# Attention and mixture of experts on one core: TensorE's work of a head pair in two rounds by array form instead of four

## The chip, the core and the metric

The kernel runs on one core of a Trainium2 chip. The metric is the device time of one execution in microseconds, given as the median over several runs. TensorE does the matrix products and writes to PSUM; VectorE, ScalarE and GpSimd read PSUM or SBUF and do the rest; SyncE issues the DMAs. Each engine takes its own instructions in the order in which they are written, and semaphores order the engines against each other. In the profile TensorE is PE, its loads of stationary operands PEld, VectorE DVE, ScalarE ACT, GpSimd POOL, SyncE SP.

## The reference

Eight sequences of 512 tokens with 128 channels go through one post-norm layer: 16 heads of width 64, then eight experts of which the router takes two.

```
q, k, v = (einsum('bsd,hdk->bhsk', x, w) for w in (w_q, w_k, w_v))
weights = softmax(einsum('bhqk,bhmk->bhqm', q, k) / 8)
z = einsum('bhqm,bhmk->bhqk', weights, v)          # heads side by side, then z @ w_o
x = layernorm(x + (x + z @ w_o))
combine = softmax of the two largest of x @ gate_w, 0 elsewhere
y = sum over e of combine[e] * (silu(x @ w1[e]) @ w2[e])
out = layernorm(x + (x + y))
```

## The kernel before

**Tiling.** Two heads form a pair, one in the partitions 0 to 63 and one in 64 to 127; 8 sequences by 8 pairs of heads make 64 pairs, n = 0 to 63. Attention runs over the pairs (the first eight and last four written out, the rest in a loop of four); the experts follow. An operand of a product is mostly a high and a low part in fp32r, so that a product is three passes. For a pair TensorE does, with the lines of its matmuls:

- `coarse(n, u, t)`, L497: the high parts of q against k, for the queries of block t (t = 0 to 3), into the two PSUM banks COARSE and COARSE+1. VectorE's `maxima(n, t)`, L961, takes the maxima out of them; there is one such pair of banks, so block t+1 waits for the maxima of block t.
- `turn_maxima(n)`, L503: a transpose of the 128x128 maxima into bank COARSE. VectorE's `shift_part(n)`, L969, makes the shift out of it.
- `scores(n, u, t)`, L521 and L527: six products of q and k for the keys of block t, and two that add the shift, into the banks 0, 1 (t even) or 2, 3 (t odd). ScalarE's `exps`, L809, turns them into probabilities.
- `times_v(n, u, c)`, L539: block c of the probabilities times v, into bank Z. `sum_probs(n)`, L552: the sums of the probabilities, by a matrix of ones, into bank MISC. Both are float32.
- `project_q(n)`, `project_k(n)`, L447 to L449: q and k of a later pair, into bank MISC; `project_v(n)`, the same lines with an xT_cur operand, v of two pairs at a time, in even pairs only, into the banks 0 and 1; `project_out(n)`, the same lines with zT_hi, the output projection, into bank MISC.

**Array forms.** The profile writes the part of TensorE's array that a matmul uses, contraction by output: coarse and scores are 64\*128 (two heads in two halves of the rows, issued as a couple, and they run side by side), times_v and sum_probs are 128\*64 (two halves of the columns), the projections and the transpose are 128\*128.

**Order around the change.** In the pass of pair n TensorE does the scores of n, coarse of n+1, times_v and sum_probs of n-1, project_q and project_k of n+2, and project_out of n-2. A list in `body` (L595 to L625) sets their order by hand. The other engines have lists of their own, which name the same steps. VectorE's list for a pass is:

```
maxima(n + 1, 0)
reciprocals(n - 1)
maxima(n + 1, 1)
q_part(n + 2, (u + 2) % TURNS)
maxima(n + 1, 2)
maxima(n + 1, 3)
k_part(n + 2, (u + 2) % TURNS)
shift_part(n + 1)
z_part(n - 1)
acc_part(n - 2)
```

`reciprocals(n - 1)` (L977 to L981: a transpose of the sums out of bank MISC into zT, a reciprocal, a transpose back) waits for `sums_done` and for `zT_lo_done`, the step that last reads zT. That is GpSimd's `zT_part(n - 2)`, L363, the first step of GpSimd's pass, before its three additions of probabilities (L359). It takes what ScalarE's `zT_part(n - 2)`, L816, wrote, and ScalarE does that one right behind the first exponential of its pass (`exps(n, j, 0)`, `zT_part(n - 2)`, `exps(n, j, 1)`, `q_part`, `exps(n, j, 2)`, `k_part`, `exps(n, j, 3)`, and `v_part` in even pairs). `q_part` and `k_part` exist on ScalarE (high part, L790 and L794) and on VectorE (low part, L948 and L953).

Of the kernel before, what the change touches and what calls it, by code (L numbers as in the profile page):

```python
# [34 lines left out]
def attention_moe_kernel(nc, x, w_q, w_k, w_v, w_o, gate_w, w1, w2, out):  # L35
# [17 lines left out]
    with ExitStack() as ctx:  # L53
# [3 lines left out]
        def sem(name):  # L57
            return ctx.enter_context(nc.semaphore(name))
# [59 lines left out]
        def carve(*shape):  # L118

            n = 1  # L120
            for d in shape:
                n *= d
            ap = free[:, carved[0]:carved[0] + n]
            carved[0] += n
            names = " ".join("abc"[:len(shape)])
            return ap.rearrange(f"p ({names}) -> p {names}", **dict(zip("abc", shape))) if len(shape) > 1 else ap
# [3 lines left out]
        before = carve(NE, NE)  # L130
# [32 lines left out]
        s = {n: sem(n) for n in names}  # L163
# [4 lines left out]
        def wait(eng, semaphore, value):  # L168

            if not isinstance(value, int) or value > 0:  # L170
                eng.wait_ge(semaphore, value)
# [45 lines left out]
        def is_first(n):  # L217
            return isinstance(n, int) and n == 0
# [9 lines left out]
        def is_last(n, ahead):  # L228
            return isinstance(n, int) and n + ahead >= PAIRS
# [205 lines left out]
        def _(pe):  # L435
# [20 lines left out]
            def project_q(m, i, j):  # L456

                if isinstance(m, int) and m < 2:
                    pe.wait_ge(s["w_split"], 1)
                    wait(pe, s["k_hi_done"], m)  # L460
                    wait(pe, s["k_lo_done"], m)
                else:
                    pe.wait_ge(wqk_cur_in[j], DMA * i)

                    pe.wait_ge(s["k_hi_done"], m)
                    pe.wait_ge(s["k_lo_done"], m)
                    wait(pe, s["sums_out"], m - 2)
                project_qk(0, m, j).then_inc(s["q_done"], 1)

            def project_k(m, j):  # L470
                if isinstance(m, int) and m < 2:
                    pe.wait_ge(s["w_split"], 2)

                pe.wait_ge(s["q_hi_done"], m + 1)
                pe.wait_ge(s["q_lo_done"], m + 1)
                project_qk(1, m, j).then_inc(s["k_done"], 1)

            def project_v(m):

                pe.wait_ge(s["xT_cur_in"], DMA * (m // 2 + 1))  # L480

                pe.wait_ge(s["exp_done"], TT * m + 3)
                for t in range(TT):
                    tok = slice(t * P, (t + 1) * P)
                    mm = product(psum[:, t // 2, t % 2 * 2 * P:(t % 2 + 1) * 2 * P], [xT_cur[:, part, tok] for part in range(2)],
                                 [w_tab[:, bass.ds(m % HP, 2), 2, part, :] for part in range(2)])
                mm.then_inc(s["vT_done"], 1)

            def coarse(n, u, t):

                if t == 0:
                    pe.wait_ge(s["q_hi_done"], n + 1)
                    pe.wait_ge(s["k_hi_done"], n + 1)
                wait(pe, s["max_done"], TT * n + t)
                for h in range(2):
                    half = slice(h * DK, (h + 1) * DK)
                    mm = nc.tensor.matmul(psum[:, COARSE + h, :], q_pair[u][half, 0, t * P:(t + 1) * P],  # L497
                                          k_pair[u][half, 0, :], start=True, stop=True)
                mm.then_inc(s["coarse_done"], 1)

            def turn_maxima(n):
                pe.wait_ge(s["max_done"], TT * (n + 1))
                nc.tensor.transpose(psum[:, COARSE, 0:P], bits(neg_max[:]), ident[:]).then_inc(s["maxT_done"], 1)  # L503

            def scores(n, u, t):

                if is_first(n) and t == 0:
                    pe.wait_ge(s["xT_lo_done"], B)
                    pe.wait_ge(s["acc_set"], B // 2)
                    pe.wait_ge(s["ones_set"], 1)  # L510
                if t == 0:
                    pe.wait_ge(s["q_lo_done"], n + 1)
                    pe.wait_ge(s["k_lo_done"], n + 1)
                wait(pe, s["exp_done"], TT * n + t - 1)
                if t == 0 and u % 2 == 1:
                    pe.wait_ge(s["v_done"], (n - 1) // 2 + 1)
                keys = slice(t * P, (t + 1) * P)
                for kp, qp in ((0, 0), (1, 0), (0, 1)):
                    for h in range(2):
                        half = slice(h * DK, (h + 1) * DK)  # L520
                        nc.tensor.matmul(psum[:, 2 * (t % 2) + h, :], k_pair[u][half, kp, keys], q_pair[u][half, qp, :],  # L521
                                         start=(kp == 0 and qp == 0), stop=False)
                if t == 0:
                    pe.wait_ge(s["shift_done"], n + 1)
                for h in range(2):
                    half = slice(h * DK, (h + 1) * DK)
                    mm = nc.tensor.matmul(psum[:, 2 * (t % 2) + h, :], ones_r[half, :],  # L527
                                          shift[half].rearrange("p t q -> p (t q)"), start=False, stop=True)
                mm.then_inc(s["scores_done"], 1)

            def times_v(n, u, c):

                if c == 0:

                    pe.wait_ge(s["exp_done"], TT * n + TT)
                    pe.wait_ge(s["v_done"], (n - u % 2) // 2 + 1)
                    wait(pe, s["z_done"], n)
                for h in range(2):
                    mm = nc.tensor.matmul(psum[h * DK:(h + 1) * DK, Z, :], v[u // 2][:, u % 2, c, h, :], probs[u % 2][:, h, c, :],  # L539
                                          start=(c == 0), stop=(c == TT - 1))  # L540
                if c == TT - 1:
                    mm.then_inc(s["pv_done"], 1)

            def sum_probs(n):

                pe.wait_ge(s["added"], (TT - 1) * (n + 1))

                pe.wait_ge(s["k_hi_done"], n + 3 if not is_last(n, 2) else PAIRS)
                pe.wait_ge(s["k_lo_done"], n + 3 if not is_last(n, 2) else PAIRS)
                wait(pe, s["acc_done"], n - 1)  # L550
                for h in range(2):
                    mm = nc.tensor.matmul(psum[h * DK:(h + 1) * DK, MISC, :], ones, probs_sum[:, h, :], start=True, stop=True)  # L552
                mm.then_inc(s["sums_done"], 1)
# [28 lines left out]
            for t in range(TT):  # L582
                coarse(0, 0, t)
# [5 lines left out]
            def body(n, u):  # L589
                j = u % 2  # L590
                ahead, project = not is_last(n, 1), not is_last(n, 2)
                former, before_former = not is_first(n), not (isinstance(n, int) and n < 2)
                after, before = (u + 1) % TURNS, (u - 1) % TURNS

                scores(n, u, 0)  # L595
                if ahead:
                    coarse(n + 1, after, 0)
                if former:
                    times_v(n - 1, before, 0)
                    sum_probs(n - 1)  # L600
                scores(n, u, 1)
                if ahead:
                    coarse(n + 1, after, 1)
                if former:
                    times_v(n - 1, before, 1)
                if project:
                    project_q(n + 2, (n + 2 - j) // 2, j)
                scores(n, u, 2)
                if ahead:
                    coarse(n + 1, after, 2)  # L610
                if former:
                    times_v(n - 1, before, 2)
                if project:
                    project_k(n + 2, j)
                if ahead:
                    coarse(n + 1, after, 3)
                scores(n, u, 3)
                if j == 0:
                    project_v(n)
                if former:  # L620
                    times_v(n - 1, before, 3)
                if ahead:
                    turn_maxima(n + 1)
                if before_former:
                    project_out(n - 2)  # L625

            loops(pe, body)

            def to_tokens(b):
# [598 lines left out]
```

## Time and profile before

| | us |
|---|---|
| median of 3 runs | 1229.1 |
| lowest and highest | 1227.48 and 1229.37 |
| the profiled execution, its own time | 1227.94 |
| its span in the profile | 1226.1 |

The span is the time from the first to the last recorded instruction; 1.8 us lie around it. The pass of an odd pair takes some 13.2 us and that of an even pair, which holds `project_v`, some 14.7 us; pairs fill the span from about 35 to 925 us, the experts the rest. In a row of the timeline the first two numbers are start and duration in us; "x6" are matmuls of one line that follow each other. The matmuls are pipelined and their ends are modelled, so that a row's duration overlaps the next row: the time that a step costs TensorE is the distance from its start to the start of what follows. A bracket at the end of a row gives the engine's idle time before it and what released it.

### The profile page before, as it was taken

The page shows a single profiled execution, that of the slowest core. Times are in us where ns is not written, and L with a number is a line of the kernel's source. Part 1 is how long each engine was busy: PE and PEld are TensorE (multiplying, and loading weights), DVE is VectorE, ACT ScalarE, POOL GpSimd, SP SyncE. Part 2 cuts the span into 40 slices and gives each one's busy share as a digit, 9 for nine tenths or more (in the row PEclk, how much of TensorE's full clock was granted, in tenths as well). Part 3 has the DMA queues.
Part 4 walks back from the last instruction along what each step waited for, and adds up shares of the span by engine and source line. Part 5 has one row for each costly group of instructions (what it writes and reads, how often), then busy time and mean ns, then how long its engine had stood idle before and what let it go on. Part 6 is the DMA issues. An engine that isn't in the chain of part 4 may idle for free. (4 is left out here: it accounts for less than half of the span.)

```text
span 1226.1 us, 18385 instructions
## 1 busy us (share of the span) xinstructions
PE 1149.8 (94%) x5912; PEld 630.2 (51%) x5912; DVE 830.1 (68%) x1170; ACT 584.1 (48%) x680; POOL 728.8 (59%) x376
## 2 busy tenths in 40 slices
PE   4899999999999999999999999999996788988886
PEld 3444445444444444544444444455443666766664
DVE  4666866667766676666676766766765676677764
ACT  4445444444444444444444444444442556555653
POOL 0476766555666566665566655666565466566665
PEclk9999999999999999999999999999999899999999
DMA  7203111111111111111111111111100000000000
GB/s 171 73 19 103 44 44 44 43 56 43 43 43 45 66 47 43 43 43 56 43 43 43 43 64 52 43 43 43 48 26 35 1 9 18 18 17 17 9 10 18
DMA packets 41326, 52.31 MB, mean 43 GB/s; under 512 B 9296, under 2 KB 27728, under 8 KB 41296
## 3 DMA queue, kind: packets, MB, share of 16 engines
q1 hardware_dynamic: 41296, 51.92, 12.2%
q8 instruction: 17, 0.28, 0.1%
q14 instruction: 13, 0.11, 0.0%
HBM read 6.30 MB, written 2.10 MB: 7 GB/s over the span
## 5 line engine op out<-in xcount | busy, mean ns | idle before, releaser
L961 DVE TENSOR_REDUCE neg_max<-psum 128x2 fp32r<-128x1024 f32 x256 | 311.5, 1217 | 95.7 <-PE psum L497 93.9
L521 PE MATMUL psum<-q_pair,k_pair 64*128 64x512 f32 x1536 | 240.4, 417 | 3.7 <-DVE xT L943 2.6
L809 ACT ACTIVATE probs_even<-psum 128x1024 f32<-128x1024 f32 x128 | 131.2, 1025 | 164.4 <-PE psum L527 164.4
L809 ACT ACTIVATE x_tok<-psum 128x1024 f32<-128x1024 f32 x128 | 131.1, 1024 | 159.1 <-PE psum L527 159.1
L394 POOL TENSOR_TENSOR k_pair<-x_tok,q_pair 128x1024 fp32r<-128x1024 f32 x64 | 152.3, 2390 | 90.2 <-ACT q_pair L904 90.2
L359 POOL TENSOR_TENSOR probs_sum<-probs_sum,probs_even 128x1024 f32<-128x1024 f32 x64 | 152.6, 2384 | 64.8 <-ACT probs_even L809 64.7
L359 POOL TENSOR_TENSOR probs_sum<-probs_sum,x_tok 128x1024 f32<-128x1024 f32 x64 | 152.7, 2386 | 64.1 <-ACT x_tok L809 63.8
L521 PEld LDWEIGHTS psum<-q_pair,k_pair 64*128 64x128 f32 x1536 | 130.0, 185 | 117.0 <-issue 97.1
L363 POOL TENSOR_TENSOR zT_lo<-zT,zT_hi 128x512 fp32r<-128x512 f32 x64 | 82.4, 1287 | 125.3 <-ACT zT_hi L816 125.3
L539 PE MATMUL psum<-probs_even,v 128*64 128x512 f32 x512 | 138.1, 618 | 0.0
L539 PE MATMUL psum<-x_tok,v 128*64 128x512 f32 x512 | 137.9, 618 | 0.0
L1143 DVE TENSOR_TENSOR x_tok<-x_tok,psum 128x1024 f32<-128x1024 f32 x64 | 77.9, 1217 | 77.3 <-PE psum L685 48.4
L359 POOL TENSOR_TENSOR probs_sum<-probs_even 128x1024 f32<-128x1024 f32 x32 | 76.5, 2392 | 79.6 <-ACT probs_even L809 79.6
L497 PE MATMUL psum<-k_pair,q_pair 64*128 64x512 f32 x512 | 110.7, 427 | 5.3 <-DVE neg_max L961 5.3
L977 DVE STREAM_TRANSPOSE zT<-psum 128x512 f32<-128x512 f32 x64 | 45.9, 717 | 96.1 <-POOL zT_lo L363 95.4
L359 POOL TENSOR_TENSOR probs_sum<-x_tok 128x1024 f32<-128x1024 f32 x32 | 76.7, 2396 | 48.4 <-ACT x_tok L809 48.4
L527 PE MATMUL psum<-shift,ones_r 64*128 64x512 f32 x512 | 101.7, 391 | 0.0
L969 DVE TENSOR_TENSOR shift<-psum,shift_mask 128x512 fp32r<-128x512 f32 x64 | 44.3, 692 | 75.1 <-PE psum L503 75.1
L897 ACT ACTIVATE x_tok<-psum 128x1024 f32<-128x1024 f32 x64 | 65.5, 1026 | 56.4 <-PE psum L449 54.0
L447 PEld LDWEIGHTS psum<-xT,wqk_cur 128*128 128x128 f32 x132 | 24.7, 187 | 103.7 <-issue 103.6
L790 ACT ACTIVATE q_pair<-psum 128x512 fp32r<-128x512 f32 x64 | 38.3, 598 | 73.2 <-PE psum L449 73.2
L695 PE MATMUL psum<-q_pair,w_tab 128*128 128x512 f32 x256 | 71.5, 401 | 1.0 <-DVE v L1152 0.7
(116 smaller groups left out, 1905.1 us busy)
## 6 DMA issues: line engine op xcount, KB each, us to landing
xT_cur<-xT SPq DMA_DIRECT2D x32, 512.0 KB, 2.9
wqk_cur<-w_tab SPq DMA_DIRECT2D x62, 256.0 KB, 2.7
wo_cur<-w_tab SPq DMA_DIRECT2D x64, 128.0 KB, 2.0
x_tok<-L_attn_x_dram SPq DMA_DIRECT2D x8, 256.0 KB, 5.3
probs_even<-acc SPq DMA_DIRECT2D x8, 256.0 KB, 2.4
out_dram<-probs_even SPq DMA_DIRECT2D x8, 256.0 KB, 2.3
acc<-L_ffn_w_dram SPq DMA_DIRECT2D x1, 1024.0 KB, 5.7
acc<-L_attn_w_q_dram SPq DMA_DIRECT2D x1, 512.0 KB, 5.1
```

Source lines behind the costliest of these rows:

```text
L359: nc.gpsimd.tensor_tensor(probs_sum[:], left, probs[j][:, :, c, :], ALU.add).then_inc(s["added"], 1)
L363: nc.gpsimd.tensor_tensor(zT_lo[:], zT[:], bits(zT_hi[:]), ALU.subtract).then_inc(s["zT_lo_done"], 1)
L394: nc.gpsimd.tensor_tensor(g_lo[e % GB], gated[e % 2], bits(g_hi[e % GB]), ALU.subtract).then_inc(s["g_lo_done"], 1)
L497: mm = nc.tensor.matmul(psum[:, COARSE + h, :], q_pair[u][half, 0, t * P:(t + 1) * P], k_pair[u][half, 0, :], start=True, stop=True)
L521: nc.tensor.matmul(psum[:, 2 * (t % 2) + h, :], k_pair[u][half, kp, keys], q_pair[u][half, qp, :], start=(kp == 0 and qp == 0), stop=False)
L527: mm = nc.tensor.matmul(psum[:, 2 * (t % 2) + h, :], ones_r[half, :], shift[half].rearrange("p t q -> p (t q)"), start=False, stop=True)
L539: mm = nc.tensor.matmul(psum[h * DK:(h + 1) * DK, Z, :], v[u // 2][:, u % 2, c, h, :], probs[u % 2][:, h, c, :], start=(c == 0), stop=(c = ...
L695: nc.tensor.matmul(psum[:, Y, :], w2_tab[:, e, f, part, :], g_hi[e % GB][:, f, :], start=(e == 0 and f == 0 and part == 0), stop=False)
L809: nc.scalar.activation(probs[j][:, :, t, :], psum[:, 2 * (t % 2):2 * (t % 2) + 2, :], ACT.Exp).then_inc(s["exp_done"], 1)
L897: nc.scalar.activation(silu[e % 2], psum[:, FC * (e % 2):FC * (e % 2 + 1), :], ACT.Silu).then_inc(s["silu_done"], 1)
L961: nc.vector.tensor_reduce(neg_max[:].rearrange("p (h k) -> p h k", h=2)[:, :, t], psum[:, COARSE:COARSE + 2, :], AX.X, ALU.max, negate=Tru ...
L1143: nc.vector.tensor_tensor(gated[e % 2], silu[e % 2], psum[:, CB, :].unsqueeze(1).broadcast_to([P, FC, S]), ALU.mult).then_inc(s["gated"], 1)
```

## The change

In `body` the order of TensorE's steps is written anew. In one pass of a pair the steps of the same array form stand together, in two rounds: coarse, two scores, coarse; then the sums and two blocks of times_v; then project_q; and again coarse, two scores, coarse; project_k and, in even pairs, project_v; two blocks of times_v; turn_maxima and project_out. Since coarse of block 0 now stands ahead of the first scores, whose wait for the shift it used to follow, it waits itself for the step that reads bank COARSE, `shift_done`. No instruction is added or left out, and the lists of the other engines are the same.

```diff
                 if t == 0:
                     pe.wait_ge(s["q_hi_done"], n + 1)
                     pe.wait_ge(s["k_hi_done"], n + 1)
+                if t == 0:
+
+                    wait(pe, s["shift_done"], n)
                 wait(pe, s["max_done"], TT * n + t)
...
-                scores(n, u, 0)
                 if ahead:
                     coarse(n + 1, after, 0)
-                if former:
-                    times_v(n - 1, before, 0)
-                    sum_probs(n - 1)
+                scores(n, u, 0)
                 scores(n, u, 1)
                 if ahead:
                     coarse(n + 1, after, 1)
                 if former:
+                    sum_probs(n - 1)
+                    times_v(n - 1, before, 0)
                     times_v(n - 1, before, 1)
                 if project:
                     project_q(n + 2, (n + 2 - j) // 2, j)
-                scores(n, u, 2)
                 if ahead:
                     coarse(n + 1, after, 2)
-                if former:
-                    times_v(n - 1, before, 2)
+                scores(n, u, 2)
+                scores(n, u, 3)
+                if ahead:
+                    coarse(n + 1, after, 3)
                 if project:
                     project_k(n + 2, j)
-                if ahead:
-                    coarse(n + 1, after, 3)
-                scores(n, u, 3)
                 if j == 0:
                     project_v(n)
                 if former:
+                    times_v(n - 1, before, 2)
                     times_v(n - 1, before, 3)
```

The changed file is three lines longer above these steps, so that L497 becomes L500, L503 L506, L521 L524, L527 L530, L539 L542 and L552 L555. TensorE's queue in the first half of the pass of pair 2, before (from the scores of block 0 to project_q):

```order
L521 MATMUL psum<-q_pair,k_pair 128x512 x6
L527 MATMUL psum<-shift,ones_r 128x512 x2
L497 MATMUL psum<-k_pair,q_pair 128x512 x2
L539 MATMUL psum<-x_tok,v 64x512 x2
L552 MATMUL psum<-probs_sum,ones_r 64x512 x2
L521 MATMUL psum<-q_pair,k_pair 128x512 x6
L527 MATMUL psum<-shift,ones_r 128x512 x2
L497 MATMUL psum<-k_pair,q_pair 128x512 x2
L539 MATMUL psum<-x_tok,v 64x512 x2
L447 MATMUL psum<-xT,wqk_cur 128x512
L448 MATMUL psum<-xT,wqk_cur 128x512
L449 MATMUL psum<-xT,wqk_cur 128x512
```

The same half pass on TensorE now, down to coarse of block 2:

```order
L500 MATMUL psum<-k_pair,q_pair 128x512 x2
L524 MATMUL psum<-q_pair,k_pair 128x512 x6
L530 MATMUL psum<-shift,ones_r 128x512 x2
L524 MATMUL psum<-q_pair,k_pair 128x512 x6
L530 MATMUL psum<-shift,ones_r 128x512 x2
L500 MATMUL psum<-k_pair,q_pair 128x512 x2
L555 MATMUL psum<-probs_sum,ones_r 64x512 x2
L542 MATMUL psum<-x_tok,v 64x512 x4
L447 MATMUL psum<-xT,wqk_cur 128x512
L448 MATMUL psum<-xT,wqk_cur 128x512
L449 MATMUL psum<-xT,wqk_cur 128x512
L500 MATMUL psum<-k_pair,q_pair 128x512 x2
```

The scores of block 2, which stood between project_q and coarse of block 2, now come behind that coarse step; between coarse of block 1 and that of block 2 there is the sum, two blocks of times_v and project_q.

TensorE's queue at the end of the pass of pair 1 (which has no project_out yet; from pair 2 on it stands behind the transpose L503) and the start of the next pass, before:

```order
L497 MATMUL psum<-k_pair,q_pair 128x512 x2
L521 MATMUL psum<-q_pair,k_pair 128x512 x6
L527 MATMUL psum<-shift,ones_r 128x512 x2
L539 MATMUL psum<-probs_even,v 64x512 x2
L503 MATMUL psum<-ident,neg_max 128x128
L521 MATMUL psum<-q_pair,k_pair 128x512 x6
L527 MATMUL psum<-shift,ones_r 128x512 x2
L497 MATMUL psum<-k_pair,q_pair 128x512 x2
```

and the same place on TensorE now, from coarse of block 3 on:

```order
L500 MATMUL psum<-k_pair,q_pair 128x512 x2
L447 MATMUL psum<-xT,wqk_cur 128x512
L448 MATMUL psum<-xT,wqk_cur 128x512
L449 MATMUL psum<-xT,wqk_cur 128x512
L542 MATMUL psum<-probs_even,v 64x512 x4
L506 MATMUL psum<-ident,neg_max 128x128
L500 MATMUL psum<-k_pair,q_pair 128x512 x2
L524 MATMUL psum<-q_pair,k_pair 128x512 x6
```

The first step of a pass is now the coarse step, which waits for the shift that comes out of the transpose (L506); before, six matmuls of the scores stood between the two.

## Rows read from the trace of the kernel before

**Rows 1.** Page, busy time of each engine in the whole span.

```profile
PE 1149.8 (94%) x5912; PEld 630.2 (51%) x5912; DVE 830.1 (68%) x1170; ACT 584.1 (48%) x680; POOL 728.8 (59%) x376
```

**Rows 2.** Stretch 600:895: length; PE, PEld, DVE, ACT, POOL busy; granted clock, DMA.

```profile
600.00:895.00 295.00, 295.00 (x1608) 144.60 (x1606) 203.22 (x254) 133.98 (x159) 177.81 (x85) 1.00 0.12 45
```

**Rows 3.** Timeline of PE, one odd pair: start, duration, engine, line, operation.

```profile
606.22 0.33 PE L503 MATMUL psum<-ident,neg_max 128*128 128x128 f32 x1
...
607.18 0.96 PE L521 MATMUL psum<-q_pair,k_pair 64*128 64x512 f32 x6
607.98 0.40 PE L527 MATMUL psum<-shift,ones_r 64*128 64x512 f32 x2
608.20 0.41 PE L497 MATMUL psum<-k_pair,q_pair 64*128 64x512 f32 x2
608.54 1.08 PE L539 MATMUL psum<-probs_even,v 128*64 128x512 f32 x4
609.45 1.03 PE L552 MATMUL psum<-probs_sum,ones_r 128*64 128x512 f32 x4
...
611.77 1.08 PE L539 MATMUL psum<-probs_even,v 128*64 128x512 f32 x4
612.78 0.50 PE L447 MATMUL psum<-xT,wqk_cur 128*128 x1
...
613.68 0.97 PE L521 MATMUL psum<-q_pair,k_pair 64*128 64x512 f32 x6
...
616.94 0.50 PE L497 MATMUL psum<-k_pair,q_pair 64*128 64x512 f32 x2
617.27 0.85 PE L521 MATMUL psum<-q_pair,k_pair 64*128 64x512 f32 x6
617.97 0.39 PE L527 MATMUL psum<-shift,ones_r 64*128 64x512 f32 x2
...
619.30 0.33 PE L503 MATMUL psum<-ident,neg_max 128*128 128x128 f32 x1
...
620.42 0.96 PE L521 MATMUL psum<-q_pair,k_pair 64*128 64x512 f32 x6
```

**Rows 4.** Timeline of PE, the even pair behind it, around project_v and its end.

```profile
631.22 0.41 PE L527 MATMUL psum<-shift,ones_r 64*128 64x512 f32 x2
631.55 0.39 PE L447 MATMUL psum<-w_tab,xT_cur 128*128 x1
...
633.18 1.08 PE L539 MATMUL psum<-x_tok,v 128*64 128x512 f32 x4
...
635.14 0.96 PE L521 MATMUL psum<-q_pair,k_pair 64*128 64x512 f32 x6
```

**Rows 5.** Timeline of ACT in the odd pair of rows 3: start, duration, operation, [idle before].

```profile
608.41 1.02 ACT L809 ACTIVATE x_tok<-psum 128x1024 f32<-128x1024 f32 x1 [2.07 <-PE psum L527]
609.34 0.62 ACT L816 ACTIVATE zT_hi<-zT 128x512 fp32r<-128x512 f32 x1
```

**Rows 6.** Timeline of POOL in the same pair.

```profile
610.03 1.28 POOL L363 TENSOR_TENSOR zT_lo<-zT,zT_hi 128x512 fp32r<-128x512 f32 x1 [2.77 <-ACT zT_hi L816]
```

**Rows 7.** Timeline of DVE in the same pair.

```profile
606.59 0.69 DVE L969 TENSOR_TENSOR shift<-psum,shift_mask 128x512 fp32r<-128x512 f32 x1 [1.98 <-PE psum L503]
...
607.80 0.68 DVE L997 TENSOR_TENSOR acc<-psum,acc 128x512 f32 x1
...
611.42 0.72 DVE L977 STREAM_TRANSPOSE zT<-psum 128x512 f32<-128x512 f32 x1 [1.55 <-POOL zT_lo L363]
...
613.10 1.19 DVE L961 TENSOR_REDUCE neg_max<-psum 128x2 fp32r<-128x1024 f32 x1
614.42 0.69 DVE L948 SCALAR_TENSOR_TENSOR q_pair<-psum,q_pair 128x512 fp32r<-128x512 f32 x1
```

**Rows 8.** Timeline of all engines, pair 62, which has no project_q or project_k.

```profile
905.92 1.19 DVE L961 TENSOR_REDUCE neg_max<-psum 128x2 fp32r<-128x1024 f32 x1
...
907.16 0.50 PE L497 MATMUL psum<-k_pair,q_pair 64*128 64x512 f32 x2 [0.44 <-DVE neg_max L961]
```

## The prediction

> **What bounds the kernel now.** I read first the busy times of the page. TensorE is busy for 94% of the span, VectorE for 68%, and the others for less [rows 1]. The share by stretch says more: between 600 and 895 us, well inside the pairs, TensorE is busy for the whole 295 us at the full granted clock, 2.4 GHz, while VectorE does 203 us [rows 2]. So in the pairs TensorE's queue sets the time, and what a pass takes is read from its timeline: the odd pass runs from 607.18 to 620.42, 13.24 us [rows 3], the even one behind it to 635.14, 14.72 us [rows 3, 4]. I write T0 for the start of a pass, C0 to C3 for coarse, S0 to S3 for scores, V0 to V3 for times_v.
>
> But the others are not far behind. One chain starts in a pass and comes back to TensorE in it: the matmuls with the shift in S0 (607.98), ScalarE's exponential (608.41) and the high part of zT behind it in its queue (609.34) [rows 5], GpSimd's low part (610.03) [rows 6], VectorE's transpose of the sums, released by it (611.42), and behind the reciprocals in VectorE's queue the maxima of block 1, 613.10 to 614.29 [rows 7]. C2 may not start before them. Before the change C2 comes late enough. Pair 62 has no projections, so less lies ahead of C2, and there the wait is in the open: the maxima end at 907.11, C2 starts at 907.16, and TensorE was idle for 0.44 us [rows 8]. That is the row on which this prediction turns.
>
> **What the change saves.** A change of form costs some 0.1 us on its way out and as much on its way in. Out: a block of times_v takes 0.91 us ahead of the sums (608.54 to 609.45) and 1.01 ahead of a projection (611.77 to 612.78). In: the six matmuls of the scores take 0.80 us (607.18 to 607.98) behind a projection and 0.70 (617.27 to 617.97) behind coarse [rows 3]. The pass without waits, from the same rows:
> - T0 to C2: C0 0.33 (616.94 to 617.27); S0 and S1 0.70 and 0.22 each (0.22 is 607.98 to 608.20), 1.84; C1 0.34 (608.20 to 608.54); sums and V0 0.91 each; V1 1.01; project_q 0.90 (612.78 to 613.68). Sum 6.24 [rows 3].
> - C2 to the next T0: C2 0.33; S2 and S3 1.84; C3 0.33, the way into a projection (631.22 to 631.55) [rows 4]; project_k 0.90; V2 0.91; V3 1.01; transpose and project_out 0.96 (606.22 to 607.18) [rows 3]. Sum 6.28.
>
> That is 12.52 us for 13.24: 0.72 saved. In an even pass project_v took 1.63 us (631.55 to 633.18) [rows 4] with a way in and out that project_k, next to it now, already has, so 1.43 is added: 13.95 for 14.72, 0.77 saved. A page has this as a rule: the Trainium skill, TensorEngine Tiling, section "Tiling Modes" (Key Properties), says that a change of tiling mode drains TensorE. The trace agrees on the sign, with its 0.1 us on either side; by that rule alone the change would be a gain, which is the first rival below.
>
> **What it adds.** Only TensorE's list is new. VectorE still does the reciprocals ahead of the maxima of block 1, and ScalarE still does zT behind the first exponential.
> - *C2.* Before, S1, C1, S2, two blocks of times_v, the sums and project_q lay between S0 and C2; now S2 has gone behind C2, and what is left is too short. S0 starts at T0 + 0.33, its shift matmuls at T0 + 1.03. From there the chain takes 6.31 us (607.98 to 614.29) [rows 3, 7] and 0.05 to TensorE (907.11 to 907.16) [rows 8], so C2 starts at T0 + 7.39 and not at 6.24: a wait of 1.15. Everything else in the pass stands behind it in TensorE's queue. Bounds: the chain might be 0.2 shorter or longer, as its steps meet other work.
> - *C0.* It waits for the shift now, which is made from the transpose at the end of the pass before. The transpose starts at 606.22, the shift ends at 607.28 [rows 3, 7]: 1.06, and 0.05 to TensorE, 1.11. Transpose and project_out cover 0.96 of it; 0.15 is left. Before, six matmuls of S0 covered it. Queued behind C0 is the whole pass. No row shows this wait with a coarse step; it lies between 0 (the shift 0.15 earlier than in its row) and 0.35 (0.2 later, the same margin as for the chain).
> - *C1.* Its bank is free when VectorE has done the shift, z, acc and the maxima of block 0. Acc ends at 608.48, 2.26 after the transpose started [rows 3, 7], so 1.15 after the new T0; with some 1.2 for the maxima and 0.05, C1 may start at T0 + 2.40 and stands at 0.33 + 1.84 = 2.17. It waits for 0.23, but that falls into C2's wait: project_q would end at 6.47, still ahead of 7.39. Its cost is nothing while the chain lasts, 0.23 if that is gone.
> - *Sums and project_q.* The sums end near T0 + 3.7. VectorE's transpose of them can't start before zT_lo, at 1.03 + 3.44 = 4.47 (607.98 to 611.42) [rows 3, 7], and project_q, which waits for it, comes at 5.57, after its end at 5.19. No wait.
> - *C3.* After the maxima of block 1 VectorE does q's low part (614.42, 0.69) [rows 7], to T0 + 8.16, and then the maxima of block 2, to 9.36. C3 stands at 7.39 + 0.33 + 1.84 = 9.56. Covered by 0.15 only.
> - *GpSimd and the last exponentials.* S3's exponential now waits behind project_k in ScalarE's queue, but the next one that wants it is the next pass's sums, over 5 us later. Nothing.
>
> **The sum.** An odd pass: -0.72 + 1.15 + 0.15 = +0.58. An even one: -0.77 + 1.30 = +0.53. With 31 odd and 30 even passes (pairs 1 to 61; 0, 62 and 63 lack steps and are left at nothing) that is 18.0 + 15.9 = 33.9 us. The profiled execution took 1227.9 (its span 1226.1), so 1261.8; the median of the runs is 1.2 higher: 1263 us. The experts come later by as much and stay as they are.
>
> A page speaks against the change as well: the Trainium skill, TensorEngine Tiling, section "Performance Considerations" (PSUM Bottleneck), says that tiling makes TensorE faster but not what takes its results out of PSUM, which may then be the bound. The wait in pair 62 is of that kind, VectorE's maxima out of PSUM [rows 8]; by this rule C2's wait is what one should expect.
>
> **The rivals.**
> - *TensorE stays the bound (faster).* If the maxima of block 1 came by T0 + 6.24, so if the chain took 1.15 us less than its row, C2 would not wait and nearly all of 31 x 0.72 + 30 x 0.77 = 45 us would be kept: 1184. The point where the change breaks even is a chain 0.6 us shorter than that. For it: TensorE waits for nothing in rows 2. Against it: pair 62, where the same chain already holds C2 up. 7 in 100; a chain just short enough for no change, 1229, 3 in 100.
> - *More waits (slower still).* C3's cover of 0.15 is thin, and C0's wait may be 0.35. If the two add 0.3 in each pass, 61 x 0.3 = 18 us come on top: 1281. For it: a late q_part moves everything behind it on VectorE. Against it: its rows add up to a time ahead of C3. 10 in 100.
> - *The change doesn't save what it says.* If a step pays its 0.1 us on either side whatever stands next to it (because of a fresh load of weights, say), the stretch from C2 on would keep some 0.3 us: 1281 again, since the first stretch is set by the chain. Against it: the 0.91 us and the 0.70 above are of steps that stand beside their like. 4 in 100.
>
> **How the numbers follow.** The forecast, 1263, has 76 in 100; its own range is 0.2 us a pass to either side, 1251 to 1275. The two heavier cases take 14, at 1281. To hold 8 in 10 the range runs from 1248 to 1284. A measurement here can tell 0.2% from no change, 2.5 us; faster by more 0.07, within it 0.03, slower by more 0.90.
>
> **What would show it.** In the trace of the changed kernel the first C2 row of every pass (the third coarse couple) should have an idle time of about 1.1 us ahead of it, released by VectorE's neg_max, and the first C0 row some 0.15 us, released by the shift; odd passes take 13.8 us, even ones 15.25; between the two waits TensorE runs without a gap, with times_v blocks of 0.91 us next to one another; in VectorE's rows the transpose of the sums is still released by zT_lo and the maxima of block 1 stand right behind the reciprocals. I am wrong if C2 has no wait, or if the idle time moves to C1, C3 or the sums and is of another size.

## The result and the profile after

The changed kernel takes 1272.4 us (median of 4 runs, 1270.6 to 1275.0) against 1228.7 us before: a ratio of 1.036, 95% interval 1.034 to 1.038. It is slower by 44 us. The forecast was 1263 us, slower by 34, with a range of 1248 to 1284. The profiled execution was the slowest of the four, 1275.0 us, with a span of 1273.2.

The page of the changed kernel, busy time of each engine and the group of the coarse matmuls (busy, mean ns, idle time before them and what ended most of it):

```profile
PE 1114.0 (87%) x5912; PEld 665.4 (52%) x5912; DVE 825.0 (65%) x1170; ACT 567.0 (45%) x680; POOL 723.6 (57%) x376
...
L500 PE MATMUL psum<-k_pair,q_pair 64*128 64x512 f32 x512 | 121.1, 461 | 84.2 <-DVE neg_max L962 66.8
```

TensorE is busy for 36 us less than in [rows 1], for the same 5912 matmuls: in the main that is the saving on changes of form, which the forecast's sums put at 45. But it now sits idle for 84 us ahead of coarse, of which VectorE's maxima ended 67 us; before, the same group had 5.3 us of idle time in the whole kernel. A stretch inside the pairs, by windows (length; PE, PEld, DVE, ACT, POOL busy; granted clock), beside [rows 2], where PE was busy throughout:

```profile
300.00:600.00 300.00, 272.78 (x1548) 149.58 (x1547) 194.91 (x246) 124.21 (x154) 170.98 (x82) 1.00 0.12 46
```

The clock stayed at 2.4 GHz, so it is not a slower TensorE; it is one that waits for 9% of the time. Where, the timeline of PE shows, an odd pass and the ends of the even one behind it (start, duration, operation, idle time before and its releaser), to be held against [rows 3, 4]:

```profile
606.43 0.33 PE L506 MATMUL psum<-ident,neg_max 128*128 128x128 f32 x1
...
607.74 0.49 PE L500 MATMUL psum<-k_pair,q_pair 64*128 64x512 f32 x2 [0.28 <-DVE shift L970]
...
608.83 0.43 PE L530 MATMUL psum<-shift,ones_r 64*128 64x512 f32 x2
...
609.99 0.44 PE L500 MATMUL psum<-k_pair,q_pair 64*128 64x512 f32 x2
610.36 1.08 PE L555 MATMUL psum<-probs_sum,ones_r 128*64 128x512 f32 x4
...
613.31 0.49 PE L447 MATMUL psum<-xT,wqk_cur 128*128 x1 [0.15 <-issue]
...
615.21 0.50 PE L500 MATMUL psum<-k_pair,q_pair 64*128 64x512 f32 x2 [0.95 <-DVE neg_max L962]
...
617.42 0.40 PE L500 MATMUL psum<-k_pair,q_pair 64*128 64x512 f32 x2
...
620.51 0.33 PE L506 MATMUL psum<-ident,neg_max 128*128 128x128 f32 x1
...
621.70 0.50 PE L500 MATMUL psum<-k_pair,q_pair 64*128 64x512 f32 x2 [0.17 <-DVE shift L970]
...
629.02 0.50 PE L500 MATMUL psum<-k_pair,q_pair 64*128 64x512 f32 x2 [0.95 <-DVE neg_max L962]
...
637.05 0.50 PE L500 MATMUL psum<-k_pair,q_pair 64*128 64x512 f32 x2 [0.28 <-DVE shift L970]
...
666.52 0.50 PE L500 MATMUL psum<-k_pair,q_pair 64*128 64x512 f32 x2 [0.28 <-DVE shift L970]
```

C0 stands at 607.74, C1 at 609.99, C2 at 615.21, C3 at 617.42. The pass takes 13.96 us (607.74 to 621.70) and the even one behind it 15.35 (to 637.05); the next two, which complete the loop's four, take 29.47 together (to 666.52). C2 has an idle time of 0.95 us ahead of it, ended by the maxima, C0 one of 0.28 or 0.17, ended by the shift; C1 and C3 have none. The steps that lead to C2, on ACT, POOL and DVE of the changed kernel, answer to [rows 5 to 7] (POOL's step takes zT and zT_hi; no row of POOL in these traces reads PSUM):

```profile
609.30 1.03 ACT L810 ACTIVATE x_tok<-psum 128x1024 f32<-128x1024 f32 x1 [3.61 <-PE psum L530]
610.22 0.62 ACT L817 ACTIVATE zT_hi<-zT 128x512 fp32r<-128x512 f32 x1
```

```profile
610.92 1.27 POOL L363 TENSOR_TENSOR zT_lo<-zT,zT_hi 128x512 fp32r<-128x512 f32 x1 [3.63 <-ACT zT_hi L817]
```

```profile
606.79 0.69 DVE L970 TENSOR_TENSOR shift<-psum,shift_mask 128x512 fp32r<-128x512 f32 x1 [2.23 <-PE psum L506]
...
612.29 0.72 DVE L978 STREAM_TRANSPOSE zT<-psum 128x512 f32<-128x512 f32 x1 [2.48 <-POOL zT_lo L363]
...
613.97 1.19 DVE L962 TENSOR_REDUCE neg_max<-psum 128x2 fp32r<-128x1024 f32 x1
```

From the shift matmuls (608.83) over the exponential, zT high, zT low and the transpose of the sums to the end of the maxima (615.16) it is 6.33 us; the row of before gave 6.31. While VectorE waited for zT low (2.48 us idle), the maxima of block 1, whose input lay ready since C1, stood in its list behind the reciprocals.

### The profile page after: what moved, and what is told of

The parts are those of the page before. It is cut to its first block and busy times, and to the rows that moved or that the text cites. A ratio compares the mean times of both kernels' runs of the same rounds, so it can differ in the third digit from the quotient of the medians.

```text
span 1273.2 us, 18435 instructions
## 1 busy us (share of the span) xinstructions
PE 1114.0 (87%) x5912; PEld 665.4 (52%) x5912; DVE 825.0 (65%) x1170; ACT 567.0 (45%) x680; POOL 723.6 (57%) x376
## 5 line engine op out<-in xcount | busy, mean ns | idle before, releaser
L524 PE MATMUL psum<-q_pair,k_pair 64*128 64x512 f32 x1536 | 227.0, 397 | 1.9 <-DVE xT L944 1.9
L500 PE MATMUL psum<-k_pair,q_pair 64*128 64x512 f32 x512 | 121.1, 461 | 84.2 <-DVE neg_max L962 66.8
L524 PEld LDWEIGHTS psum<-q_pair,k_pair 64*128 64x128 f32 x1536 | 148.6, 186 | 27.1 <-DVE xT L944 2.4
L500 PEld LDWEIGHTS psum<-k_pair,q_pair 64*128 64x128 f32 x512 | 50.3, 186 | 155.1 <-DVE neg_max L962 106.2
L542 PE MATMUL psum<-x_tok,v 128*64 128x512 f32 x512 | 123.3, 602 | 0.0
L542 PE MATMUL psum<-probs_even,v 128*64 128x512 f32 x512 | 122.8, 600 | 0.0
L530 PE MATMUL psum<-shift,ones_r 64*128 64x512 f32 x512 | 104.9, 393 | 0.0
```

## The experiments

**The list of VectorE, one step.** If the chain holds C2, taking the maxima of block 1 out of it must free C2, with TensorE's list as it is.

```diff
-                if former:
-                    reciprocals(n - 1)
                 if ahead:
                     maxima(n + 1, 1)
+                if former:
+                    reciprocals(n - 1)
                 if project:
                     q_part(n + 2, (u + 2) % TURNS)
```

> The changed kernel; on VectorE the maxima of block 1 stand ahead of the reciprocals instead of behind them, nothing else. Theory (the chain first exponential, zT high, zT low, reciprocals, maxima of block 1 holds C2 up): the wait of 0.95 to 1.15 us ahead of C2 is gone; C3 now waits some 0.5 us, because q's low part stands ahead of the maxima of block 2 in VectorE's queue; an odd pass takes about 13.4 us for 14.06, the kernel about 1235 us (1228 to 1245). Rival (TensorE's steps themselves have become slower in the new order): no change, 1272 us.

Measured: 1241.3 us, ratio to the kernel before 1.011 (1.009 to 1.013). C2 and C3 of an odd pass in this run:

```profile
624.41 0.50 PE L500 MATMUL psum<-k_pair,q_pair 64*128 64x512 f32 x2
...
627.02 0.51 PE L500 MATMUL psum<-k_pair,q_pair 64*128 64x512 f32 x2 [0.27 <-DVE neg_max L962]
```

The wait ahead of C2 is gone. C3 waits instead, 0.25 to 0.35 us where 0.5 was expected, for the maxima of block 2 behind q's low part, and an odd pass takes 13.45 or 13.57 us, where 13.4 was expected. The forecast of this run was 6 us too low, the rival's "no change" is out.

**The list of VectorE, two steps.** On top of that, the maxima of block 2 ahead of q's low part:

```diff
                 if former:
                     reciprocals(n - 1)
+                if ahead:
+                    maxima(n + 1, 2)
                 if project:
                     q_part(n + 2, (u + 2) % TURNS)
                 if ahead:
-                    maxima(n + 1, 2)
                     maxima(n + 1, 3)
```

> The changed kernel; on VectorE the maxima of block 1 ahead of the reciprocals and the maxima of block 2 ahead of q's low part. Theory: C2 and C3 wait for next to nothing; left are C0 (0.15 to 0.3) and C1 (0.2); an odd pass takes about 12.95 us, an even one 14.4, the kernel 1209 us (1203 to 1217), faster than before the change by about as much as the changes of form cost. Rival (the time goes to TensorE's steps, not to the wait): 1272 us.

Measured: 1211.2 us, ratio 0.987 (0.985 to 0.988), so faster than before the change, and 61 us faster than the changed kernel whose TensorE list it has. DVE of this run:

```profile
612.41 1.23 DVE L962 TENSOR_REDUCE neg_max<-psum 128x2 fp32r<-128x1024 f32 x1 [0.59 <-PE psum L500]
614.23 0.72 DVE L978 STREAM_TRANSPOSE zT<-psum 128x512 f32<-128x512 f32 x1 [0.59 <-POOL zT_lo L363]
...
616.67 1.23 DVE L962 TENSOR_REDUCE neg_max<-psum 128x2 fp32r<-128x1024 f32 x1 [0.69 <-PE psum L500]
```

The maxima of block 1 now run in the time in which VectorE waited for zT low, which still releases the reciprocals, and the maxima of block 2 wait for C2, no longer C2 for the maxima. Odd passes take 12.9 to 13.05 us, even ones 14.3 to 14.4. What is left is mainly C0's wait for the shift, 0.16 to 0.28 us.

**The same list of VectorE under TensorE's old order.** Is the gain the new VectorE list, whatever TensorE does? The kernel before, with this edit alone:

```diff
-                if former:
-                    reciprocals(n - 1)
                 if ahead:
                     maxima(n + 1, 1)
+                if former:
+                    reciprocals(n - 1)
+                if ahead:
+                    maxima(n + 1, 2)
                 if project:
                     q_part(n + 2, (u + 2) % TURNS)
                 if ahead:
-                    maxima(n + 1, 2)
                     maxima(n + 1, 3)
```

> The kernel before, TensorE's order in four rounds, with VectorE's new order (maxima of blocks 1 and 2 ahead of reciprocals and q's low part). Theory: TensorE was the bound there and waited for nothing, so VectorE's order alone is worth nothing: passes of 13.25 and 14.7 us, 1229 us (1225 to 1232). Rival (VectorE's order is the gain by itself, whatever TensorE's order is): as fast as the changed kernel with the same VectorE order.

Measured: 1365.7 us, ratio 1.113 (1.111 to 1.115). Not as fast, and not the same either: 137 us slower than before. Both the theory and the rival are out, and PE of this run says why:

```profile
605.91 0.49 PE L447 MATMUL psum<-xT,wqk_cur 128*128 x1 [1.18 <-DVE zT L977]
...
610.23 0.47 PE L447 MATMUL psum<-xT,wqk_cur 128*128 x1 [1.00 <-DVE q_pair L948]
```

In the old order coarse of block 1 comes behind the sums, so with the new list the transpose of the sums, which project_q waits for, stands behind maxima that start later than the sums are there; in the same way project_k waits for q's low part behind the maxima of block 2. The two waits, 1.03 to 1.18 and 1.00 us, stand in nearly every pass. Each list fits one order of TensorE: crossed one way they lose 137 us, the other way (the changed kernel) 44.

**The chain, shorter and longer.** Two runs change nothing but the place of zT high in ScalarE's list, ahead of the first exponential or behind the second.

```diff
+                if not (isinstance(n, int) and n < 2):
+                    zT_part(n - 2)
                 exps(n, j, 0)
-                if not (isinstance(n, int) and n < 2):
-                    zT_part(n - 2)
```

> The changed kernel; on ScalarE the high part of zT stands ahead of the first exponential of the pass instead of behind it. Theory (the chain runs through that exponential): zT low ends some 1.9 us earlier, VectorE's transpose of the sums is then released by the sums, some 0.6 us earlier than now, and the wait ahead of C2 falls from about 1.0 to 0.4 us; odd pass 13.5 us, kernel about 1238 us (1230 to 1248). Rival (the reciprocals are held by the sums, not by zT): nothing moves, 1272 us.

Measured: 1242.3 us, ratio 1.012 (1.010 to 1.014). Expected was 1238. DVE and PE of this run:

```profile
607.83 0.72 DVE L978 STREAM_TRANSPOSE zT<-psum 128x512 f32<-128x512 f32 x1 [1.71 <-PE psum L555]
```

```profile
610.75 0.50 PE L500 MATMUL psum<-k_pair,q_pair 64*128 64x512 f32 x2 [0.44 <-DVE neg_max L962]
```

The transpose of the sums is now released by the sums (L555), and C2's idle time is 0.34 to 0.44 us, as expected. Odd passes fall to 13.24 to 13.34 us, below the expected 13.5; the two passes in which VectorE also sets up the second half of acc give some of it back, 19.7 and 18.9 us for 17.2 and 16.1. The other way:

```diff
                 exps(n, j, 0)
-                if not (isinstance(n, int) and n < 2):
-                    zT_part(n - 2)
...
                 exps(n, j, 1)
+                if not (isinstance(n, int) and n < 2):
+                    zT_part(n - 2)
```

> The changed kernel; on ScalarE the high part of zT stands behind the second exponential of the pass instead of the first, so the chain is one exponential longer (0.93 us). Theory: C2 waits 0.93 us longer in each of 61 passes, kernel about 1329 us (1315 to 1340). Rival (C2's wait is set by the sums or by TensorE): little or nothing, 1272 to 1285 us.

Measured: 1353.7 us, ratio 1.101 (1.098 to 1.105), where 1329 was expected. Most passes are longer by what was expected: an odd one takes 15.0 us for 14.06 and an even one 16.3 for 15.3, 0.94 us each. The idle time grows ahead of project_q, though, and not ahead of C2 as expected: project_q waits 0.84 to 1.09 us for the transpose of the sums, the step of the chain before the maxima, and C2 0.95 as before. The rest is in about one pass in four, which takes 1.5 us more than that. Windows of PE in this run (length, busy time, granted clock):

```profile
676.00:679.00 3.00, 1.69 (x7) 1.00 0.00 0
679.00:682.00 3.00, 2.51 (x14) 0.71 0.00 0
...
694.00:697.00 3.00, 1.37 (x5) 1.00 0.00 0
697.00:700.00 3.00, 2.58 (x12) 0.55 0.00 0
```

Behind the two waits of a pass (project_q for the transpose, then C2), in which PE is busy for about half of 3 us, the granted clock fell towards the lower level, 1.2 GHz, in some passes and stayed at 2.4 GHz in others (busy 1.54 of 3 us at 646 to 649, clock 1.00 behind it). So a wait can cost more than it lasts. The expectation had the chain right and left this out.

**C0 behind the scores again.** The wait for the shift is the change's only new wait in the code. This run keeps coarse and scores together but swaps the first two, so that six matmuls cover the shift.

```diff
+                scores(n, u, 0)
                 if ahead:
                     coarse(n + 1, after, 0)
-                scores(n, u, 0)
                 scores(n, u, 1)
```

> The changed kernel; in TensorE's list the scores of block 0 stand ahead of coarse of block 0 again, so the shift is covered by six matmuls; coarse and scores stay together. Theory: C0's wait for the shift is gone (0.2 us a pass), the chain to C2 starts at T0 and not 0.33 later, C1 now waits some 0.6 us for the maxima of block 0, but inside the time in which C2 would wait anyway: odd pass about 13.5 us, even 14.8, kernel about 1240 us (1230 to 1250). Rival (each wait of TensorE costs what it lasts): C1's wait comes on top, 1272 to 1290 us.

Measured: 1253.6 us, ratio 1.021 (1.020 to 1.023): faster than the changed kernel, by 19 us and not by 32. C0's wait is gone; odd passes take 13.55 us, as expected, even ones 15.0 where 14.8 was expected, and the longer of the two passes with the second half of acc takes 18.5 us for 17.2. PE and DVE of this run:

```profile
613.12 0.49 PE L500 MATMUL psum<-k_pair,q_pair 64*128 64x512 f32 x2 [0.41 <-DVE neg_max L962]
...
617.68 0.50 PE L500 MATMUL psum<-k_pair,q_pair 64*128 64x512 f32 x2 [0.45 <-DVE neg_max L962]
```

```profile
614.76 0.72 DVE L978 STREAM_TRANSPOSE zT<-psum 128x512 f32<-128x512 f32 x1 [1.70 <-PE psum L555]
```

C1 now waits 0.41 us, which pushes the sums back, and the sums, no longer zT low, release the transpose: a second way into the same chain, some 0.15 us later than zT low would have released it. C1's wait was said to be free; here about 0.25 us of it are, and the rest moves C2.

**What a change of form costs by itself.** In the kernel of the two VectorE steps, where TensorE hardly waits, coarse of block 3 goes behind project_k: one change of form more in odd passes, two in even ones.

```diff
                 scores(n, u, 3)
-                if ahead:
-                    coarse(n + 1, after, 3)
                 if project:
                     project_k(n + 2, j)
+                if ahead:
+                    coarse(n + 1, after, 3)
```

> The kernel of e2_recip_q_later, whose TensorE hardly waits, with coarse of block 3 moved behind project_k: one change of array form more in an odd pass (scores, projection, coarse, times_v), two more in an even one, no instruction added. It measures what a change of form costs by itself. Theory (0.2 us a change, half on the way out, half on the way in): 0.2 us more in odd passes and 0.4 in even ones, some 18 us in all, 1229 us (1222 to 1236). Rival (a step pays its start and end whatever stands beside it): 1211 us as before.

Measured: 1238.4 us, ratio 1.007 (1.006 to 1.009): 27 us more than without the swap, where 18 were expected. PE of this run, an even pass and the odd one behind it (coarse of block 0, from the last shift matmuls to times_v, the next coarse of block 0):

```profile
601.51 0.50 PE L500 MATMUL psum<-k_pair,q_pair 64*128 64x512 f32 x2
...
609.77 0.39 PE L530 MATMUL psum<-shift,ones_r 64*128 64x512 f32 x2
610.33 0.47 PE L447 MATMUL psum<-xT,wqk_cur 128*128 x1 [0.16 <-DVE q_pair L949]
...
613.24 1.94 PE L542 MATMUL psum<-x_tok,v 128*64 128x512 f32 x8
...
616.41 0.51 PE L500 MATMUL psum<-k_pair,q_pair 64*128 64x512 f32 x2 [0.28 <-DVE shift L970]
...
624.81 0.39 PE L530 MATMUL psum<-shift,ones_r 64*128 64x512 f32 x2
...
626.66 1.94 PE L542 MATMUL psum<-probs_even,v 128*64 128x512 f32 x8
...
629.83 0.51 PE L500 MATMUL psum<-k_pair,q_pair 64*128 64x512 f32 x2
```

and the same two passes of the kernel without the swap:

```profile
582.42 0.50 PE L500 MATMUL psum<-k_pair,q_pair 64*128 64x512 f32 x2 [0.16 <-DVE shift L970]
...
590.66 0.39 PE L530 MATMUL psum<-shift,ones_r 64*128 64x512 f32 x2
...
593.52 1.94 PE L542 MATMUL psum<-x_tok,v 128*64 128x512 f32 x8
...
596.70 0.50 PE L500 MATMUL psum<-k_pair,q_pair 64*128 64x512 f32 x2 [0.28 <-DVE shift L970]
...
605.12 0.39 PE L530 MATMUL psum<-shift,ones_r 64*128 64x512 f32 x2
...
606.56 1.94 PE L542 MATMUL psum<-probs_even,v 128*64 128x512 f32 x8
...
609.74 0.50 PE L500 MATMUL psum<-k_pair,q_pair 64*128 64x512 f32 x2 [0.28 <-DVE shift L970]
```

The even pass takes 14.90 us for 14.28, the odd one 13.42 for 13.04. The same matmuls from the shift to times_v take 3.47 us for 2.86 in the even pass and 1.85 for 1.44 in the odd one. Of each difference 0.16 is a new wait of project_k for q's low part (in the odd pass the same 0.16 stands ahead of 625.36); what is left is 0.45 us for two changes of form and 0.25 for one. That is near the expected 0.4 and 0.2. The new wait, which the expectation left out, makes some 10 us over 61 passes, and with it the 18 come to the 27. The rival, that a step pays the same wherever it stands, is out.

**Better versions.** With the two VectorE steps, the transpose of the maxima goes ahead of the last two blocks of times_v in even passes, where project_v with the same form stands before it:

```diff
+                if ahead and j == 0:
+                    turn_maxima(n + 1)
                 if former:
                     times_v(n - 1, before, 2)
                     times_v(n - 1, before, 3)
-                if ahead:
+                if ahead and j == 1:
                     turn_maxima(n + 1)
```

> The changed kernel with VectorE's order of e2_recip_q_later, and in even passes the transpose of the maxima ahead of the last two blocks of times_v (behind project_v, which has its array form) instead of behind them. Theory: the shift is then hidden in even passes, which lose their wait ahead of the next C0 (0.2 to 0.3 us): about 7 us less than e2_recip_q_later's 1211, 1204 us (1199 to 1209). Rival (the wait for the shift is covered by a later wait anyway): 1211 us.

Measured: 1198.8 us, ratio 0.976 (0.974 to 0.978), 12 us less than without it, where 7 were expected. Even passes, at whose end the wait for the shift is gone, take 14.0 to 14.1 us for 14.3 to 14.4, and odd ones, which begin without it, 12.85 to 12.95 for 12.9 to 13.05. With zT high ahead of the first exponential as well:

```diff
+                if not (isinstance(n, int) and n < 2):
+                    zT_part(n - 2)
                 exps(n, j, 0)
-                if not (isinstance(n, int) and n < 2):
-                    zT_part(n - 2)
```

> As e6_turn_early, and on ScalarE the high part of zT ahead of the first exponential. In e2_recip_q_later project_q still comes some 0.2 us late behind VectorE's transpose of the sums, which zT low releases. Theory: that goes, 0.2 us in most passes, and some 5 us are lost in the passes that split the experts' weights: 1200 us (1192 to 1208). Rival (project_q is late for another reason): as e6_turn_early or slower.

Measured: 1197.9 us, ratio 0.975 (0.974 to 0.977): the same as the version before it. Half of the odd passes fall to 12.7 us and half of the even ones to 13.9, but the second of the two passes with the second half of acc takes 18.0 us for 15.2, and some 2 us more go behind the last pair.

## Why the prediction was right, and where it was short

**What bounds the pass: right.** The row of pair 62 carried the argument [rows 8], and every steady pass now looks like it: C2 starts 0.05 us behind the end of the maxima of block 1 (615.16 to 615.21). Taking the maxima out of the chain removed the wait, shortening the chain shortened it, and lengthening the chain by 0.93 us lengthened a pass by 0.94.

**The saving: right.** C2 to the next transpose takes 5.30 us (615.21 to 620.51); the forecast, 6.28 less the last 0.96, is 5.32. In the last version odd passes take 11.49 and 11.66 us from C0 to the transpose; with the forecast's 0.96 for transpose and project_out that is 12.45 and 12.62, around the forecast's 12.52. The rule of the Trainium skill, TensorEngine Tiling, section "Tiling Modes" (Key Properties), on the drain at a change of mode agrees with it: 0.45 us for two changes in an even pass. Not all of the 0.72 saved in an odd pass is form, though. At its end in the kernel before, project_out stands 0.25 us behind the transpose (619.30 in [rows 3]), not 0.09 as in the even pass, because it waits for k's low part, which ends at 619.30:

```profile
618.62 0.68 DVE L953 TENSOR_TENSOR k_pair<-psum,k_pair 128x512 fp32r<-128x512 f32 x1
```

```profile
619.55 0.47 PE L447 MATMUL psum<-zT_hi,wo_cur 128*128 128x512 f32 x1
```

So 0.16 of the 0.72 was a wait that PE's modelled busy time hid, and "TensorE waits for nothing" was not quite so.

**C2: right.** C2 was to start at T0 + 7.39; it starts at 7.47 (odd) and 7.32 (even). The Trainium skill, TensorEngine Tiling, section "Performance Considerations" (PSUM Bottleneck), names the kind of bound, results that wait to be taken out of PSUM; but VectorE was busy for only 65% of the span, and it was the order of its list that made it late, not its work.

**C0: the term that was too small.** The forecast took 0.05 us from VectorE's end to TensorE's start, as measured for the maxima. For the shift it is 0.26 (607.48 to 607.74) or 0.14 (621.56 to 621.70). Transpose to C0 takes 1.31 us in three of the loop's four passes and 1.19 in the first, not 1.11. Less the 0.96 that covers it, the wait is 0.35 or 0.23 us where 0.15 was forecast: inside the stated bounds, 0 to 0.35, but at their upper end.

**C1, sums, project_q, C3: the cost right in the steady passes, two details not.** C1 was to wait for 0.23 us at no cost and has no idle time: C0 itself stands later behind the transpose than forecast, and C1 with it. The transpose of the sums is released by zT low, and C3 has no idle time, as forecast. project_q was to have no wait and has one of 0.15 us in odd passes: it starts 0.30 us behind the end of the transpose of the sums (613.01 to 613.31), a latency that the forecast left out. That is T0 + 5.57, the forecast's own figure, by luck: the wait of C1 that was to bring it there did not come, and this one did. It ends ahead of C2 all the same and costs nothing. How much room C1 has can be estimated from the run with the scores first, where the transpose of the sums starts 1.21 us behind the sums (613.55 to 614.76): in the changed kernel the sums would release it at 611.57, zT low does at 612.29, so C1 could wait for some 0.7 us before it cost anything.

**The sum: 10 us short.** Two passes together take 29.31 us (607.74 to 637.05) and the next two 29.47 (to 666.52), for 27.96 before, so +1.43 on the mean where the forecast had 0.58 + 0.53 = 1.11. Over 61 passes that is 44 us for 34, and nearly all of the difference is C0's term: 0.17 us a pass on the mean, the 1.31 and 1.19 above for 1.11. The other 3 us of the profiled execution's 47 come from places that the forecast left at the steady price or at nothing. In the pass that starts at 133.76 VectorE has work on the second half of acc (L1042) ahead of the maxima of block 0:

```profile
134.62 2.51 DVE L1042 SCALAR_TENSOR_TENSOR acc<-xT,acc 128x512 f32<-128x512 f32 x2
137.05 1.21 DVE L962 TENSOR_REDUCE neg_max<-psum 128x2 fp32r<-128x1024 f32 x1
```

```profile
138.32 0.79 PE L500 MATMUL psum<-k_pair,q_pair 64*128 64x512 f32 x2 [2.08 <-DVE neg_max L962]
```

C1 waits for those maxima, the sums stand behind C1, and the pass takes 17.2 us (to the C0 at 150.93). Before, with C1 later, the pass with the same work took 13.8 us. And in pair 62 C2 waits for 2.09 us, after which the granted clock falls; windows of PE in the changed kernel:

```profile
950.00:954.00 4.00, 1.91 (x16) 1.00 0.00 0
954.00:957.00 3.00, 3.00 (x15) 0.50 0.00 0
```

For 3 us the clock is at half, 1.2 GHz, and the two matmuls of the shift take 0.42 us there (954.96 to 955.38) for 0.24 just before (953.59 to 953.83). Beyond the steady +0.7 the two passes with the second half of acc (pairs 7 and 8) cost 3.4 us and pair 62 1.9 in all; the start of the kernel gives back 1.5 (the pass of pair 1 starts at 45.64 for 47.10).

## What to carry to other kernels

When the order of one engine is rewritten to save time on that engine, write down for each wait what stood between its releaser and the waiting step, and count what is left; a step that hid a chain of four engines moved away here, and for 0.7 us saved in a pass came 1.4 us of waiting. The lists of the other engines belong to the order: the same change, with two steps of VectorE's list moved, is 1.3% faster than before, and with the transpose moved too 2.4%. Look for a place in the trace of before where the cover is already missing (a last pass, a pass without some step): its rows show the wait and its latency before the change is made.

## What was not expected

- VectorE's new list under TensorE's old order costs 137 us, 11%; the old list under the new order costs 44, 4%. Each is good with its partner only.
- The time from the end of a step on VectorE to the matmul on TensorE that waits for it is not one number, but keeps to one for each step: 0.05 us for the maxima to coarse, 0.15 for q's low part to project_k, 0.25 for k's low part to project_out, 0.30 for the transpose of the sums to project_q. The shift to coarse takes 0.26, and 0.14 in the first of the loop's four passes alone. Why they differ no run here shows.
- Waits of about 1 us, two of them close together, stood in some passes ahead of a granted clock of 0.55 to 0.71 on the mean of the next 3 us; in others, with as little work, it stayed at 1.00.
